# Feed-forward tiles of a decoder layer: GpSimd normalises and rounds x, and the rounded x is transposed between the halves of the down projection

## The reference

```python
def _layernorm(x, axis=-1, eps=1e-05):
    m = jnp.mean(x, axis=axis, keepdims=True)
    v = jnp.var(x, axis=axis, keepdims=True)
    return (x - m) / jnp.sqrt(v + eps)
...
def _weight_quant(w):
    scale = 1.0 / jnp.clip(jnp.mean(jnp.abs(w)), 1e-05)
    wq = jnp.clip(jnp.round(w * scale), -1.0, 1.0) / scale
...
def _act_quant(x):
    scale = 127.0 / jnp.clip(jnp.max(jnp.abs(x), axis=-1, keepdims=True), 1e-05)
    xq = jnp.clip(jnp.round(x * scale), -128.0, 127.0) / scale
...
gate = jax.nn.silu(_bitlinear(x, w_gate))      # w_gate, w_up: (2048, 512)
up = _bitlinear(x, w_up)
return _bitlinear(gate * up, w_down)           # w_down: (512, 2048)
...
x = x + _L0_ffn_ref(_layernorm(x, axis=-1), L0_ffn_w_gate, L0_ffn_w_up, L0_ffn_w_down)
```

## Time and profile before

| | |
|---|---|
| Time of three runs | 1396.25, 1397.2, 1398.44 us: median 1397.2 |
| The profiled execution | 1394.94 us, span 1393.0 us, so 1.94 us lie around the span |
| Busy in the span | PE 1236.3 us (89%), DVE 859.3 (62%), ACT 562.3 (40%), POOL 167.0 (12%) |
| Feed-forward part | from about 1157 us to the end, 236 us |
| Granted PE clock in it | 0.72 from 1157 to 1213 us, 1.00 from 1213 to 1367 us |

### The profile page before, as it was taken

The page is one execution under the profiler, slowest core; times in us unless marked ns, Lnnn a source line. Parts: engine busy times, 40 slices in busy tenths (PEclk is TensorE's granted clock), DMA queues, the critical chain, the costliest instruction groups (busy, mean ns, idle before and its releaser), DMA issues. The chain is left out here.

```text
span 1393.0 us, 27044 instructions
## 1 busy us (share of the span) xinstructions
PE 1236.3 (89%) x10602; PEld 953.6 (68%) x10602; DVE 859.3 (62%) x1554; ACT 562.3 (40%) x923; POOL 167.0 (12%) x244
## 2 busy tenths in 40 slices
PE   4799989993799999999999999999999973599997
PEld 3687868882677887787887778777878753344443
DVE  5766646654456566566566565565665545788884
ACT  2222222231234334344343334343343334477775
POOL 0011111114001010110111011011101011001110
PEclk9999999996799999999999999999999995999999
DMA  5222242223234243343243341532432218212211
GB/s 157 86 73 86 75 155 89 84 101 112 68 105 104 48 131 82 72 120 96 62 122 81 96 122 45 134 89 66 113 87 68 65 30 291 114 53 68 62 64 40
DMA packets 69142, 129.52 MB, mean 93 GB/s; under 512 B 12720, under 2 KB 25136, under 8 KB 68512
## 3 DMA queue, kind: packets, MB, share of 16 engines
q1 hardware_dynamic: 65880, 117.19, 29.8%
q0 software_dynamic: 3168, 11.01, 2.3%
HBM read 68.96 MB, written 11.22 MB: 58 GB/s over the span
## 5 line engine op out<-in xcount | busy, mean ns | idle before, releaser
L1146 DVE TENSOR_REDUCE xa_m_part<-xa_psM 112x1 f32<-112x376 f32 x512 | 265.5, 546 | 227.7 <-PE xa_psM L1297 223.7
L1073 ACT ACTIVATE space<-xa_psS 125x448 f32<-125x448 f32 x384 | 207.4, 545 | 251.3 <-PE xa_psS L1281 248.0
L1297 PE MATMUL xa_psM<-xa_k,xa_q 104*112 104x376 f32 x512 | 156.2, 350 | 9.5 <-DVE xa_m_part L1146 6.4
L1281 PE MATMUL xa_psS<-xa_q,xa_k 104*125 104x224 f32 x768 | 144.4, 271 | 0.5 <-ACT space L1073 0.5
L1281 PEld LDWEIGHTS xa_psS<-xa_q,xa_k 104*125 104x125 f32 x768 | 136.7, 187 | 7.4 <-issue 1.1
L1321 PE MATMUL xa_psO<-space,cv 125*32 125x224 f32 x1536 | 110.1, 359 | 1.3 <-ACT space L1073 1.3
L1321 PE MATMUL xa_psO<-space,ones 125*32 125x224 f32 x1536 | 107.8, 352 | 0.0
L1297 PEld LDWEIGHTS xa_psM<-xa_k,xa_q 104*112 104x112 f32 x512 | 88.5, 176 | 27.7 <-DVE xa_m_part L1146 11.1
L1267 PE MATMUL xa_psR<-xa_cT_hi,w_hi 128*128 128x376 f32 x256 | 88.2, 344 | 10.0 <-DVE xa_cT_lo L1136 7.7
L1267 PE MATMUL xa_psR<-xa_cT_hi,w_lo 128*128 128x376 f32 x256 | 90.7, 354 | 0.0
L1267 PE MATMUL xa_psR<-xa_cT_lo,w_hi 128*128 128x376 f32 x256 | 87.7, 343 | 0.0
(11 more groups left out here) (197 smaller groups left out, 2574.3 us busy)
## 6 DMA issues: line engine op xcount, KB each, us to landing
xa_k<-xa_k_st SPq DMA_DIRECT2D x384, 94.0 KB, 2.2
cv<-in_ctx_dram SPq DMA_DIRECT2D x8, 1500.0 KB
xa_q<-xa_q_st SPq DMA_DIRECT2D x192, 56.0 KB, 2.0
cv<-in_L_ffn_w_gate_dram SPq DMA_DIRECT2D x8, 512.0 KB, 4.9
cv<-in_L_ffn_w_up_dram SPq DMA_DIRECT2D x8, 512.0 KB, 6.1
cv<-in_L_ffn_w_down_dram SPq DMA_DIRECT2D x8, 512.0 KB, 6.9
ff_w_raw<-in_L_ffn_w_gate_dram SPq DMA_DIRECT2D x4, 1024.0 KB, 9.1
ff_w_raw<-in_L_ffn_w_up_dram SPq DMA_DIRECT2D x4, 1024.0 KB, 14.1
```

The costliest lines, as they stand in the source:

```text
L1073: nc.scalar.activation(pT[:, (s + i) % 2, j], psS[0:KB, (HG * i + j) % NB, 0:2 * N], ACT.Exp).then_inc(exp_done, 1)
L1146: V.tensor_reduce(m_part[:, seg, t, jj:jj + 1], psM[0:T, seg, 0:SEG], AX.X, ALU.max, negate=True).then_inc(mx_read, 1)
L1281: last = M.matmul(psS[0:KB, (HG * i + j) % NB, a * N:(a + 1) * N], k4[0:ROWS, s % 2, j, col:col + KB], q4[0:ROWS, s, j, :], start=True, st ...
L1297: M.matmul(psM[0:T, seg, 0:SEG], q4[0:ROWS, g, jj, t * T:(t + 1) * T], k4[0:ROWS, g % 2, jj, seg * SEG:(seg + 1) * SEG], start=True, stop= ...
```

## The change

On POOL, `normalise` and `round_x` (`xn`, `xm`, `xq`: three instructions of 128x512) are added behind `rstd` and ahead of `store`. On DVE these three go away; `x_big` and the three steps to `x_scale` stay there, and move behind `hidden(i + 1, 1)`. On PE `turn_x` moves from ahead of the second `turn_hidden` to between the two halves of `down`. On ACT the copy of the turned x moves behind the second copy of the turned hidden values.

```diff
+            def normalise(i):
+                if not is_first(i):
+                    pool.wait_ge(xm_ready, i)
+                wait_apart(pool, x_rstd, i + 1, pool_passed)
+                nc.gpsimd.tensor_scalar(xn[:], x_raw[:], x_mv[:, 0:1], x_rs[:], ALU.subtract, ALU.mult).then_inc(xn_ready, 1)
+
+            def round_x(i):
+                wait_apart(pool, x_scale_ready, i + 1, pool_passed)
+                nc.gpsimd.tensor_scalar(xm[:], xn[:], x_scale[:], MAGIC, ALU.mult, ALU.add).then_inc(xm_ready, 1)
+                if not is_first(i):
+                    pool.wait_ge(xq_turned, i)
+                wait_apart(pool, xm_ready, i + 1, pool_passed)
+                nc.gpsimd.tensor_scalar(xq[:], xm[:], MAGIC, QMAX, ALU.subtract, ALU.min).then_inc(xq_ready, 1)
+                pool.wait_ge(xq_ready, i + 1)
...
-            rstd(0)
-            rstd(1)
+            for i in range(2):
+                rstd(i)
+                normalise(i)
+                round_x(i)
             with pool.Fori(0, TILES - 2) as i:
                 rstd(i + 2)
+                normalise(i + 2)
+                round_x(i + 2)
                 store(i)
...
                 silu(i + 1, 3)
+                copy_turned_h(i, 1)
                 if prep:
                     copy_turned_x(i + 2)
-                copy_turned_h(i, 1)
...
-            def normalise(i):
-                dve.wait_ge(x_meanvar, i + 1)
-                dve.wait_ge(x_rstd, i + 1)
-                V.tensor_scalar(xn[:], x_raw[:], x_mv[:, 0:1], x_rs[:], ALU.subtract, ALU.mult).then_inc(xn_ready, 1)
+            def largest_x(i):
                 dve.wait_ge(xn_ready, i + 1)
                 V.tensor_reduce(x_big[:], xn[:], AX.X, ALU.max, apply_absolute_value=True).then_inc(x_big_ready, 1)
...
-                dve.wait_ge(x_scale_ready, i + 1)
-                V.tensor_scalar(xm[:], xn[:], x_scale[:], MAGIC, ALU.mult, ALU.add).then_inc(xm_ready, 1)
-                dve.wait_ge(xm_ready, i + 1)
-                wait_count(dve, xq_turned, i)
-                V.tensor_scalar(xq[:], xm[:], MAGIC, QMAX, ALU.subtract, ALU.min).then_inc(xq_ready, 1)
...
-            normalise(1)
+            largest_x(1)
+            scale_x(1)
             hidden(0, 1)
-            round_x(1)
             finish_weight(2)
...
                 hidden(i + 1, 0)
-                if prep:
-                    normalise(i + 2)
                 hidden(i + 1, 1)
                 if prep:
-                    round_x(i + 2)
+                    largest_x(i + 2)
+                    scale_x(i + 2)
                 hidden(i + 1, 2)
...
             def body(i, prep):
                 for c in range(3):
                     gate_up(i + 1, c)
                 turn_hidden(i, 0)
                 gate_up(i + 1, 3)
+                turn_hidden(i, 1)
+                down(i, 0)
                 if prep:
                     turn_x(i + 2)
-                turn_hidden(i, 1)
-                down(i)
+                down(i, 1)
```

More of the change, by code:

```diff
@@ L1620, in scale_of, with scale_x @@
                 V.tensor_scalar(scale, inv, QMAX, None, ALU.mult).then_inc(scale_ready, 1)
-            def round_x(i):
+            def scale_x(i):
                 scale_of(i, x_big[:], x_amax[:], x_inv[:], x_scale[:], x_big_ready, x_amax_ready, x_inv_ready, x_scale_ready)
-                dve.wait_ge(x_scale_ready, i + 1)
-                V.tensor_scalar(xm[:], xn[:], x_scale[:], MAGIC, ALU.mult, ALU.add).then_inc(xm_ready, 1)
-                dve.wait_ge(xm_ready, i + 1)
-                wait_count(dve, xq_turned, i)
-                V.tensor_scalar(xq[:], xm[:], MAGIC, QMAX, ALU.subtract, ALU.min).then_inc(xq_ready, 1)
             def dequantisers(i):
@@ L1701, in _ @@
             statistics(0)
-            normalise(0)
-            round_x(0)
+            largest_x(0)
+            scale_x(0)
             finish_weight(0)
@@ L1781, in turn_hidden, with down @@
                 last.then_inc(h_turned, 1)
[L1783 to L1790, removed]
+            def down(i, half):
+                if half == 0:
+                    wait_count(pe, y_ready, i)
+                pe.wait_ge(hq_T_ready, 2 * i + half + 1)
+                for m in range(HALF):
+                    k = half * HALF + m
+                    last = M.matmul(psY[:], hq_T[:, k], down_T[:, k], start=k == 0, stop=k == IT - 1)
+                if half == 1:
+                    last.then_inc(y_full, 1)
             def body(i, prep):
@@ L1818, in _ @@
                 turn_hidden(TILES - 1, half)
-            down(TILES - 1)
+            for half in range(2):
+                down(TILES - 1, half)
 def decoder_layer(nc, x, context, Wq, Wk, Wv, Wo, G1, G2, gamma, beta, theta, w_q, w_kv, w_proj, w_rel,
```

## The result

| | median | ratio to before, 95% interval |
|---|---|---|
| before | 1397.82 us (1396.25 to 1400.57, 6 runs) | |
| changed | 1391.44 us (1388.37 to 1392.18, 6 runs) | 0.9949 [0.9934, 0.9964] |

The change makes the kernel 0.5% faster, where no change was forecast. A later comparison of the same kernel gave 0.9966 [0.9954, 0.9979], so 0.3 to 0.5%.

The account below looks back on a forecast made before the run. Bound: the loop's chain through VectorE's x work, making PE wait. Profiled 1394.94 - 1.2 (loop) + 1.9 (before it) = 1395.6; with the median 2.3 above, 1397.2 + 0.7 = 1397.9 us. Range: 1387.8, less the uncertainty before the loop, to 1407.

Parts of the forecast that it names:

- The tile as it was: Feed-forward loop before: 12.54 us per tile, PE's own work 11.5, about 1.0 us waiting on VectorE's x chain.
- The formula: Loop tile through POOL's chain after the change: 9.46 + 2c us, 12.44 against 12.54, -1.2 us over 12 tiles.
- c: Time of one 128x512 instruction on POOL, taken as 1.49 us, bounds 0.775 and 1.77.
- Covers c up to 2.2: In the loop, xn on POOL starts at about 1245.2, x_big asks at 1247.4: hidden for c up to 2.2.
- What c is: Step pricing POOL's 128x512 instruction from a 224-column TENSOR_SCALAR row of 775 ns: 1.49 us.
- The straight line: POOL instruction cost: 0.22 us for one column plus 2.49 ns per further column, 1.49 us for 512.
- 512 columns are not cheaper than 224: Lower bound on c for POOL's instructions: 0.775 us.
- the case of the forecast: POOL's chain in the loop with c from 1.15 to 1.65, chance 0.45; faster by 0.2% needs c under 1.36.
- Before the loop: DVE and POOL hinder each other around weight roundings in tiles 0 and 1: +1.9 us, from 0 to 3.
- a little earlier: SP loads the next x when xn is read, now slightly sooner; costed at nothing.
- The second rival: POOL's xm and xq slower, between x_scale and the turn of x: 1405.1 us at c = 1.77; chance 0.33 for c above 1.65.
- the first (PE the bound, 11.76 per tile, 1387.8): Rival: POOL quick enough, c under 1.15, PE bounds the loop tile: -9.4 us, 1387.8 us; chance 0.22.

Follow-up runs that it names:

- the run with xq as multiply-add: Changed kernel with GpSimd's xq made as xm x 1 + (-MAGIC), without the upper limit: 1384.81 us, 0.9916; again 1385.66 us, 0.9915.
- PE's part alone: Kernel of before with only PE's and ACT's reordering, xn, xm, xq staying on VectorE: 0.9972; again 1391.79 us, 0.9958.
- GpSimd's part alone: Changed kernel with PE and ACT back in the old order, GpSimd's and VectorE's part kept: 1.0206 of before, +28 us.

## Why the prediction was wrong

**The tile as it was.** 12.54 us with the chain through VectorE's x work, PE's own work 11.5, and 11.76 as PE's bound after the change: right; the bound was met at 11.74 once nothing else held the tile, in the run with xq as multiply-add.

**The formula.** 9.46 + 2c stood for the chain through POOL. With the measured xm and xq, 0.69 + 1.93 = 2.62, it gives 12.08; measured 12.16. The product of chunk 1 came 1.04 us earlier in the tile, 0.97 was worked out; the scale came at 7.01 us, 0.17 later than worked out. Of this about 0.1 is the first step of the scale, which now stands directly behind the reduction that it reads (0.72 from start to start, where 0.61 was carried over), and 0.1 the reduction's wait for xn. "Covers c up to 2.2" was therefore slightly off: xn started 3.79 us into the tile and not 3.7, the reduction was due at 5.8 and not 5.9, and 2.08 us did not quite fit between.

**The step that failed** is "What c is": one price, 1.49 us, for two instructions, from a row with one operation. Two of them were 2.62 us together and not 2.98, which is 0.36 x 12 = 4.3 us of the forecast's error of 6.5. The longer way to the scale gives 1 us of it back, so the loop as a whole explains 3.4. Another 0.9 is the work before the loop, below; the rest lies in what differs between executions (where the part begins, the clock in the last tile, and which execution of before was profiled). The straight line itself held: a single multiply over 512 columns takes 1.50. What no row showed is that the pair multiply, add takes about half of that (0.62 to 0.77), and the other pairs tried 0.4 to 0.6 more. The bound "512 columns are not cheaper than 224" was false across forms: 0.69 against 775 ns. Whether the change was to be seen at all hung on this: c averages 1.31 over xm and xq, in the case of the forecast, but in the part of it (under 1.36) that was named as faster.

**The page of the Trainium skill** (GPSIMD Engine Reference, section 3.1) gives 769 ns for 512 elements at best. That is near multiply-add, whose 0.62 to 0.77 us are even below it, and it fits no other form measured here. The prediction weighed it against one row and dropped it for all.

**Before the loop** I counted +1.9 us. The profile has +1.0, a second one of the same kernel +2.0, and two of PE's part alone are 2.1 us apart; so the term is neither confirmed nor refuted. The mechanism was half right. POOL's instructions were stretched by weight roundings (xq 2.24, xn 3.02) while single roundings kept their 1.23; only the four in a row grew, 4.62 to 5.26. The Trainium skill (SBUF — State Buffer, "SBUF: two separate sides") says that whichever of the two starts first holds the pair of ports for its whole instruction, and that the other fully blocks. At 1169.57 and 1185.19 POOL had started first and VectorE's rounding ran through in its usual 1.23 us, so here the measurement decides against that wording. In the earlier trace rows it was VectorE that took longer, beside a TENSOR_TENSOR of POOL and not a TENSOR_SCALAR; whether that is the reason was not tried. SP's queue behind xn was costed at nothing, "a little earlier": in fact it is later everywhere. In the loop the load of x is issued 6.04 us into the tile, where it was 4.99, and VectorE asks for this x only 7.6 us after that; for the first tile it is issued 1.5 us later. No time was seen to hang on it.

**What pays.** The prediction put the gain down to PE no longer queueing behind x, and that held: PE's part alone has all of it, GpSimd's part alone costs 28 us, and the two together are no faster than the first (1392.01 and 1391.79 us on one chip). What it did not see is the second loop, over VectorE's run, the rounding and the silu, that closes at 12.1 when x stays on VectorE. Taking x off VectorE opens that one (its run to the rounding is then 1242.05 - 1233.79 = 8.26 us and no longer 9.02), and POOL's xq at 1.93 closes another at the same length; that the two lengths agree is chance. With a quick xq both are open, and another 6 to 7 us come.

**The second rival** (slower from c = 1.54 on) was not met; the first (PE the bound, 11.76 per tile, 1387.8) was not met by this change. The run with xq as multiply-add met its tile, 11.74, and came out 2 to 3 us lower in time, 1384.8 and 1385.7.

## What to carry to other kernels

Moving an instruction to another engine is priced by its exact form: measure the pair of operations, since two instructions of one name and shape differed by a factor of three, and rewriting subtract-min as multiply-add (possible where the limit is never reached) was worth as much as the whole change. When two parts of a change act on one loop, run each alone: here one had all the gain and the other only made room for a third. After a wait is removed, look for the next closed loop over the engines (here VectorE's run, ACT's rounding, the silu), not only at the engine that waited.

## What the runs showed of the hardware

GpSimd's TENSOR_SCALAR over 128x512: multiply-add 0.62 to 0.77 us, one operation 1.50, four other pairs 1.92 to 2.07. Beside weight roundings of VectorE they took longer (xm 1.48, xq 2.24, xn 3.02), while single roundings kept their 1.23 us. A wait of 2.43 us per tile on PE was followed, in four of twelve tiles, by a down projection at a lower granted clock (15 matmuls in 5.09 us, not 3.40), so that the order with this wait cost 28 us where the longer tiles at full clock make 22; in the other loops, where PE waits 0.71 us at a time at most, the clock stayed at 1.00 from 1229 to 1355 us.
